# Two wide cross-attentions whose probabilities are turned by a DMA transpose, and smaller sums and weights in two small attention layers

## The reference, cut to what matters

```python
# l1x (8 key heads, each used twice)          # l3x
q = x @ Wq                                    # q = rmsnorm(x @ Wq, gq); k = rmsnorm(ctx @ Wk, gk)
scores = q @ k.T / sqrt(128)
attn = softmax(scores)                        # 128 x 128 for each batch and head
out = (attn @ v) @ Wo
```

```python
q = rope(x @ Wq + bq); k = rope(x @ Wk + bk); v = x @ Wv + bv
att = softmax(where(mask, einsum('bhgnd,bhsd->bhns', qg, k) / sqrt(d), -inf))
y = (att @ v) @ Wo + bo
```

## Time and profile before

| | us |
|---|---|
| median of 3 runs | 3186.46 (3185.35 to 3189.64) |
| profiled execution | 3178.78 |
| its span | 3177.0 |
| busy: PE, DVE, ACT, POOL | 2808.8, 2260.2, 1880.5, 1712.1 |

### The profile page before, as it was taken

How to read it: one execution, slowest core, us unless ns; L and a number is a source line. 1 busy time by engine, 2 the same in 40 slices (tenths; PEclk the granted TensorE clock), 3 DMA queues, 4 the chain that set the end, 5 groups by cost and what they waited for, 6 DMA issues and landing times. The chain is left out here.

```text
span 3177.0 us, 72083 instructions
## 1 busy us (share of the span) xinstructions
PE 2808.8 (88%) x25739; PEld 2153.6 (68%) x25739; DVE 2260.2 (71%) x5489; ACT 1880.5 (59%) x3629; POOL 1712.1 (54%) x1840
## 2 busy tenths in 40 slices
PE   7969999798999885896787899899999799998998
PEld 5757775456888565674565555688888677776665
DVE  5567764675888632885786677677777688888787
ACT  3346763355667422564676556466666588886675
POOL 2122211223555455554874376688888598887800
PEclk9989999799999976998899999999999999999999
DMA  4010001000000444000001632000000000001000
GB/s 165 1 23 12 13 11 67 7 1 8 10 7 5 140 119 97 6 6 23 16 16 28 241 92 69 3 1 0 0 0 0 6 9 5 5 5 47 24 1 27
DMA packets 94943, 104.66 MB, mean 33 GB/s; under 512 B 40492, under 2 KB 81900, under 8 KB 91759
## 3 DMA queue, kind: packets, MB, share of 16 engines
q1 hardware_dynamic: 90104, 96.09, 9.7%
q0 software_dynamic: 4608, 5.57, 1.1%
HBM read 80.84 MB, written 13.71 MB: 30 GB/s over the span
## 5 line engine op out<-in xcount | busy, mean ns | idle before, releaser
L2232 PE MATMUL bank<-l3a_ln_xnT,far 128*128 128x128 f16 x3072 | 194.4, 220 | 1.8 <-POOL l3a_ln_xnT L2046 1.8
L2232 PEld LDWEIGHTS bank<-l3a_ln_xnT,far 128*128 128x128 f16 x3072 | 181.7, 99 | 3.3 <-POOL l3a_ln_xnT L2046 2.2
L877 PE MATMUL bank<-l2f_xnT,l2f_wi 128*128 128x512 f16 x672 | 156.5, 381 | 7.0 <-POOLq L741 6.4
L3569 PE MATMUL bank<-l0x_v,l0x_pT 128*128 128x128 f32 x1024 | 134.7, 280 | 3.2 <-ACT l0x_pT L3997 1.5
L3569 PEld LDWEIGHTS bank<-l0x_v,l0x_pT 128*128 128x128 f32 x1024 | 127.7, 193 | 13.8 <-issue 4.7
L1226 PE MATMUL bank<-l3f_xnT,near 128*128 128x512 f16 x480 | 120.6, 389 | 6.9 <-DVE l3f_xnT L1011 3.5
L3163 POOL TENSOR_TENSOR l1x_prob<-l1x_prob,l1x_srec 128x512 f32<-128x512 f32 x64 | 66.6, 1041 | 105.7 <-DVE l1x_srec L2926 105.7
L1241 PE MATMUL bank<-near,l3f_h 128*128 128x256 f16 x960 | 119.0, 274 | 4.7 <-DVE l3f_h L1016 2.1
L877 PEld LDWEIGHTS bank<-l2f_xnT,l2f_wi 128*128 128x128 f16 x672 | 65.2, 98 | 77.8 <-POOLq L741 9.9
L1241 PEld LDWEIGHTS bank<-near,l3f_h 128*128 128x128 f16 x960 | 94.0, 98 | 33.8 <-DVE l3f_h L1016 4.0
L3857 DVE TENSOR_REDUCE l0x_smax<-bank 128x4 f32<-128x512 f32 x128 | 86.2, 685 | 32.7 <-PE bank L3511 30.5
(11 more groups left out here) (743 smaller groups left out, 9404.7 us busy)
## 6 DMA issues: line engine op xcount, KB each, us to landing
far<-in_l1f_in SPq DMA_DIRECT2D x32, 256.0 KB, 3.9
l2f_front<-l2f_shares SPq DMA_DIRECT2D x5, 1024.0 KB, 4.4
sums<-near SPq DMA_DIRECT2D x2, 2176.0 KB, 18.7
far<-in_l1f_down SPq DMA_DIRECT2D x32, 128.0 KB, 4.2
far<-sums SPq DMA_DIRECT2D x8, 512.0 KB, 7.4
l2f_wi<-in_l2f_in SPq DMA_DIRECT2D x14, 256.0 KB, 6.1
far<-l0x_kT SPq DMA_DIRECT2D x64, 48.0 KB
far<-l2x_kT SPq DMA_DIRECT2D x32, 96.0 KB
```

The costliest lines, as they stand in the source:

```text
L877: last = nc.tensor.matmul(bank[:, :], wi16[n % 2][p][:, a, k, :], xnT[q][:, k, 512 * g:512 * g + 512], start=(k + p + q == 0), stop=(k == ...
L2232: last = nc.tensor.matmul(bank[:, P * j:P * j + P], w(k, 512 * c + P * j, P, p), norm.xnT[u][q][:, k, :], start=(k + p + q == 0), stop=(k ...
L3569: last = nc.tensor.matmul(b_o[:, at:at + P], pT[f % 3][:, j, :], v_all[b % NV][:, hv:hv + P], start=True, stop=True)
```

## The change

In both wide layers the probabilities stay the way they lie and are split before they are turned: `p16` holds upper and lower halves side by side (128 x 1024 float16), and SP issues one DMA transpose a chunk, of all eight blocks, from `p16` to `pT`, both with two buffers. TensorE's four float32 transposes and their PSUM bank go.

In l1x the split is made from `prob` in SBUF: ScalarE rounds (`upper_probs`), GpSimd subtracts (`lower_probs`), VectorE's subtraction goes. In l3x the exponentials go to PSUM bank 6 (`b_p`), one bank for all chunks, and give their row sums by the accumulator output; VectorE takes reciprocals, multiplies inside the bank, ScalarE rounds and VectorE subtracts from the bank; GpSimd's `divide` and VectorE's sum go. The exponentials of a chunk now wait until the chunk before has been split.

In l1a the 16 query heads' weights and bias are summed to 4 before use, so 192 columns are projected, and the rotation is three instructions. In l2x the reciprocals, the products and the offsets of the two halves are one instruction each instead of two.

In the diff, the pieces are in the order of the code: buffers, SP, TensorE, VectorE, ScalarE, GpSimd, then `small_attention_layer`.

```diff
-        b_p, b_kT = (core.bank[6:8], None) if merged else (core.bank[6:7] * 2, core.bank[7])
+        b_p, b_kT = core.bank[6:8]
-        q32, prob = sb("q32", [P, 512]), two("prob")
+        q32, prob = sb("q32", [P, 512]), two("prob") if merged else [b_p, b_p]
-        pT = [two(f"pT{u}", 512, F16) for u in range(2)]
+        p16 = [sb(f"p16{u}", [P, 2 * HC, P], F16) for u in range(2)]
+        pT = [sb(f"pT{u}", [P, 2 * HC, P], F16) for u in range(2)]
...
+                    if pr:
+                        b, u, c_, f = pr
+                        sp.wait_ge(p_split, f + 1)
+                        sp.sem_inc(p_cleared, 1)
+                        since(sp, o_made, f - 1)
+                        sp.sem_inc(p_cleared, 1)
+                        sp.dma_start_transpose(pT[c_ % 2][:, :, :], p16[c_ % 2][:, :, :].rearrange("p h k -> p (h k)")
+                                               ).then_inc(p_turned[c_ % 2], 16)
...
                 def heads_out(it):
                     b, u, c_, f = it
-                    pe.wait_ge(pT_lo, f + 1)
+                    pe.wait_ge(p_turned[c_ % 2], turns(b, c_) + 16)
...
+                    nc.vector.reciprocal(srec[c_ % 2][:, :], ssum[c_ % 2][:, :])
+                    dve.drain()
+                    nc.vector.tensor_tensor(heads(b_p[:, :]), heads(b_p[:, :]),
+                                            srec[c_ % 2][:, :].unsqueeze(2).to_broadcast(wide), ALU.mult
+                                            ).then_inc(p_ready, 1)
...
                     else:
                         kk, kt = behind(b, u, c_, K_K, NC), behind(b, u, c_, K_T, NC)
+                        if pr:
+                            lower_probs(pr)
                         if sc:
                             negated_max(sc)
...
-                        if pr:
-                            keep_probs(pr)
                         if kt:
                             query_squares(kt)
...
                 def exponentials(it):
                     b, u, c_, f = it
                     act.wait_ge(d_ready if merged else less_ready, f + 1)
-                    since(act, p_turned, f - 1)
+                    since(act, p_split, f - 1 if merged else f)
...
-                        last = nc.scalar.activation(prob[c_ % 2][:, at], b_s[:, at], ACT.Exp,
-                                                    bias=less[c_ % 2][:, j:j + 1], scale=q_rr[c_ % 2][:, j:j + 1])
+                        last = nc.scalar.activation(b_p[:, at], b_s[:, at], ACT.Exp,
+                                                    bias=less[c_ % 2][:, j:j + 1], scale=q_rr[c_ % 2][:, j:j + 1],
+                                                    accum_out=ssum[c_ % 2][:, j:j + 1])
...
+                def upper_probs(it):
+                    b, u, c_, f = it
+                    act.wait_ge(p_ready, f + 1)
+                    since(act, p_turned[c_ % 2], turns(b, c_))
+                    nc.scalar.copy(p16[c_ % 2][:, 0:HC, :], heads(prob[c_ % 2][:, :])).then_inc(p_hi, 1)
...
+                        if pr:
+                            lower_probs(pr)
                         if ex:
                             divide(ex)
...
-    QW = 384 if causal else D
+    QW = {"summed": 192, "grouped": 384}.get(kind, D)
...
+                def sum_groups(to, w):
+                    nc.vector.tensor_reduce(to[:, 0:64].rearrange("p (h d) -> p h d", h=4),
+                                            w[:, 0:D].rearrange("p (h g d) -> p h d g", h=4, g=4), AX.X, ALU.add)
+                    nc.vector.tensor_copy(to[:, 64:], w[:, D:])
...
-                    for i, (tok, ready) in enumerate(((q_tok[b % 2], q_ready), (k_tok[b % 2], k_ready))):
-                        nc.vector.tensor_tensor(tok[:, :, :], four(raws[b % 2][:, :])[:, i, :, :], sb_[:, i, :, :], ALU.add
-                                                ).then_inc(ready, 1)
+                    nc.vector.tensor_tensor(tok[b % 2][:, :, :].rearrange("p (a h) d -> p a h d", a=2),
+                                            four(raws[b % 2][:, :]), sb_, ALU.add).then_inc(q_ready, 1)
```

More of the change, by code:

```diff
@@ L2662, in context_attention_layer @@
         two = lambda n, w=512, dtype=F32: [sb(f"{n}{i}", [P, w], dtype) for i in range(2)]
-        q32, prob = sb("q32", [P, 512]), two("prob")
+        q32, prob = sb("q32", [P, 512]), two("prob") if merged else [b_p, b_p]
         qT = [two(f"qT{u}", 512, F16) for u in range(2)]
-        pT = [two(f"pT{u}", 512, F16) for u in range(2)]
+        p16 = [sb(f"p16{u}", [P, 2 * HC, P], F16) for u in range(2)]
+        pT = [sb(f"pT{u}", [P, 2 * HC, P], F16) for u in range(2)]
+        p_hi, p_split, p_cleared = sem("p_hi"), sem("p_split"), sem("p_cleared")
+        c_freed = sem("c_freed")
+        p_turned = [sem(f"p_turned{u}") for u in range(2)]
         oT = [two(f"oT{u}", 512, F16) for u in range(2)]
-        smax, ssum = sb("smax", [P, HC]), sb("ssum", [P, HC])
+        smax, ssum = sb("smax", [P, HC]), two("ssum", HC)
         srec = two("srec", HC)
@@ L2725, in _, with slot @@
                 load(1, 1)
-                with sp.Fori(1, NB // 2) as i:
-                    for u in range(2):
-                        sp.wait_ge(c_split, 2 * i + u - 1)
-                        load(2 * i + u, u)
+                def slot(b, u, c_):
+                    pr = behind(b, u, c_, K_P, NC)
+                    if c_ == 0 and behind(b, u, c_, 0, NC) and not (isinstance(b, int) and b < 2):
+                        sp.wait_ge(c_split, b - 1)
+                        sp.sem_inc(c_freed, 1)
+                        load(b, u)
+                    if pr:
[6 more added lines that the diff above has]
+                                               ).then_inc(p_turned[c_ % 2], 16)
+                run_slots(sp, slot, NC, 2, K_O)
             @block.tensor
@@ L2739, in merge @@
                         last.then_inc(m_made, 1)
-                def turn_probs(it):
-                    b, u, c_, f = it
-                    pe.wait_ge(p_ready, f + 1)
-                    since(pe, pT_lo, f - 1 if merged else f)
-                    for j in range(HC):
-                        last = nc.tensor.transpose(b_p[c_ % 2][:, P * j:P * j + P], prob[c_ % 2][:, P * j:P * j + P],
-                                                   core.ident[:, :])
-                    last.then_inc(p_turned, 1)
                 def squares(it):
@@ L2819, in heads_out @@
                     for p, q in HALVES:
-                        last = nc.tensor.matmul(b_o[:, :], c16[u][p][:, :], pT[c_ % 2][q][:, :],
+                        last = nc.tensor.matmul(b_o[:, :], c16[u][p][:, :],
+                                                pT[c_ % 2][:, HC * q:HC * q + HC, :].rearrange("p h k -> p (h k)"),
                                                 start=(p + q == 0), stop=(p == 1))
@@ L3130, in slot @@
                         if pr:
[L3131 removed]
+                            upper_probs(pr)
                     else:
@@ L3165, in divide, with lower_probs @@
                                             ).then_inc(p_ready, 1)
+                def lower_probs(it):
+                    b, u, c_, f = it
+                    pool.wait_ge(p_hi, f + 1)
+                    nc.gpsimd.tensor_tensor(p16[c_ % 2][:, HC:, :], heads(prob[c_ % 2][:, :]), p16[c_ % 2][:, 0:HC, :],
+                                            ALU.subtract).then_inc(p_split, 1)
                 def split_squares(it):
@@ L3368, in small_attention_layer @@
         if kind != "axial":
-            raws = [sb(f"raw{u}", [P, 512 if split else 384]) for u in range(2)]
+            raws = [sb(f"raw{u}", [P, 512 if split else QW]) for u in range(2)]
         if kind in ("grouped", "split"):
@@ L3639, in weights_part @@
                         centre(keys, 32)
+                    if kind == "summed":
+                        for k in range(KD):
+                            sum_groups(wide_w["q"][:, k, :], weights["q"][:, k, :])
                     dve.drain().then_inc(centred, 1)
@@ L3871, in keep_out @@
                     first = n * (g % R) if rounds > 1 else 0
[L3872 to L3874 removed]
+                    o = b_o[:, 0:n * W].rearrange("p (h a w) -> p h a w", h=n, a=parts)
+                    nc.vector.reciprocal(orec[:, 0:n, :], o[:, :, :, HD])
                     dve.drain()
```

107 lines of the change are left out of this document (46 added, 61 removed).

## The result

| | us |
|---|---|
| before, median of 4 runs beside it | 3185.90 (3175.82 to 3189.64) |
| after, median of 4 runs | 3237.93 (3232.92 to 3241.9) |
| ratio | 1.0168, 95% interval 1.0140 to 1.0195 |
| profiled execution after, its span | 3238.48, 3236.7 |

The changed kernel is 52 us slower. Forecast were 3236, with a range of 3160 to 3325, and "slower" with 0.81.

A forecast was written before the change was run, and what follows sets the result against it. It took TensorE to bound l1x and ScalarE, with all four engines 86 to 94% busy, to be critical in l3x. l3x +75, l1x -12, l1a -7, l2x -6 gave +50 on 3186.46: 3236 us, range 3160 to 3325.

The forecast's parts named there:

- l3x, ScalarE and VectorE: In l3x, ScalarE's exponentials wait 1.75 us more behind VectorE's subtraction and maximum; 7.27 us a chunk, +75 us with accumulator.
- The accumulator: Accumulator output of l3x's exponentials: +10 us, between free and 29, since summed beside a pass that runs anyway.
- The term of the waits: In l3x, 1.75 us more wait before exponentials, the 0.73 for transposes gone: 1.02 a chunk, +65 us over 64 chunks.
- l1x: the mechanism: In l1x, transposes leave full TensorE, part returns as a wait for the layer norm's lower half: -12 us.
- -31 for the transposes: In l1x, 64 float32 transposes of 0.49 us leave TensorE, the bound engine: 31 us gained.
- +19 for the norm's half: In l1x, GpSimd's new instruction delays the layer norm's lower half, so TensorE's first projection waits 1.16 us in 16 batches.
- The DMA: Transposing DMA of 256 KB lands in 3.9 us, up to 14.4 if serial; at 3.9 it does not bound l1x.
- DMA + 4.0: In l1x, the ring that closes over two chunks takes the DMA's time plus 4.0 us: 3.95 a chunk.
- the point from which it decides: DMA time from which its ring bounds l1x: 2 x 4.77 - 4.0 = 5.5 us.
- rival of a partly serial DMA: DMA takes 7.2 us, l1x 5.6 a chunk, +53 instead of -12; total +115, 3301 us; chance 0.13.
- The serial estimate of 10.5 us: Eight blocks transposed one after another by DMA: l1x 7.2 us a chunk, some 158 us more than before.
- Small layers: l1a -7 us by a narrower projection, l2x -6 by merged instructions; together -13, between 0 and -19.
- TensorE's clock: Rival: in l3x the clock falls to 1.2 GHz at 74% busy, 226 us longer, 3462; chance 0.04.

The follow-up runs named there:

- max_first: Changed kernel, but VectorE in l3x makes maximum and bias before subtracting the rounded probabilities from the bank; 3195.22 us, ratio 1.0032 to the kernel before.
- dve_sums: Changed kernel, but l3x's exponentials have no accumulator output and VectorE reduces the bank for the row sums; 3225.89 us, ratio 1.0147 to the kernel before.
- norm_early: Changed kernel, but GpSimd in l1x makes the next batch's layer norm lower half ahead of its division; 3218.45 us, ratio 1.0120 to the kernel before.
- l1x_old: Changed kernel with only l1x put back to its form before the change; 3254.56 us, ratio 1.0204 to the kernel before.
- small_old: Changed kernel with all small attention layers put back to their form before the change; 3247.73 us, ratio 1.0196 to the kernel before.
- twice: Changed kernel with every transposing DMA preceded by an identical, waited-for one into an unread buffer; 3323.47 us, ratio 1.0442 to the kernel before.

## Why the prediction was right

**l3x, ScalarE and VectorE: right.** It said 1.75 us more between rounding and exponentials, and 7.27 a chunk without accumulators. The distance is 2.19 where 2.24 was put together from rows of before, and the wait that goes (0.73) and the one that comes (1.60) are where it put them. Its own arithmetic closes: ScalarE's 5.52, with 0.38 for the accumulators and 1.60 of wait, is 7.50, and 7.48 was measured. max_first shows the order as the cause of 44 us: the instructions are the same and only VectorE's queue differs. dve_sums has 7.21 a chunk without accumulators, close to the 7.27, but with a longer VectorE slot.

**The accumulator: undersized.** +10 was taken between 0 and 29, with the reason that the sum is made beside a pass that runs anyway. That reason failed: the reading is an instruction of its own behind each activation. It measures 0.38 us a chunk, 24 over the layer, near the upper bound. The term was 14 us too small. The term of the waits was about as much too large: without the accumulators' 0.38 a chunk grew by 7.48 - 0.38 - 6.30 = 0.80 us, 51 us in 64, where 1.02 and 65 were forecast (the chunk of before was taken as 6.25 where it is 6.30, so 0.05 of the 0.22 is that). That l3x came out at +77 against +75 is therefore luck: two errors of some 14 us cancel.

**l1x: the mechanism right, both terms too large.** -31 for the transposes is -23.6 (330.4 to 306.8), which norm_early shows alone. In the middle of the layer it is 0.45 a chunk, 29 us in 64; part of the rest goes at the layer's end, where TensorE waits 2.9 us for the last transposes in norm_early. +19 for the norm's half is +16.8. The sum is -6.8 against -12.

**The DMA: right where it mattered.** 3.1 us for 3.9, DMA + 4.5 for DMA + 4.0, and the point from which it decides is 2 x 4.57 - 4.5 = 4.6 us, not 5.5. Twice the landing time goes beyond it, and l1x loses 81 us. So the rival of a partly serial DMA had its place right, and it fell on the duration. The serial estimate of 10.5 us, from the 1309 ns of the Trainium skill's "VectorE: DVE Perf Modes", section "The three transpose paths", is refuted for this form, eight blocks in one instruction: 3.1 us. By the Trainium skill's page "Advanced Engine Details and Errata", section "X-Bar Transpose (TRN2)", transposing DMAs are as fast as ordinary ones. The trace agrees as far as it goes: 256 KB transposed from SBUF to SBUF land after 3.1 us, and 256 KB of weights loaded the ordinary way after 3.9; no run has an ordinary move by the same route.

**Small layers: right in sign, too large.** -13 was forecast, between 0 and -19; undone, they cost 9 us. l1a is -7.8 in the mean (-7 forecast). The 54 matmuls of 10.3 us are now 48 of 5.4. l2x is -4.0 (-6 forecast), but l2f gives 3.5 back, which no step of the prediction had; over the eleven executions it is -2.8 and +2.7.

**TensorE's clock: nearly right.** No stretch of l3x fell to 1.2 GHz for long, but there are short ones (a mean of 0.97 in 2560 to 2860, where it was 1.00 before). The timeline of TensorE and a window over the same place, after the change:

```profile
2705.39 0.82 PE L2797 MATMUL bank<-near,l3x_cT 128*128 128x512 f16 x3 [1.93 <-DVE l3x_k_tok L2977]
...
2707.25 2.77 PE L2841 MATMUL bank<-near,l3x_oT 128*128 128x256 f16 x12
...
2714.18 1.47 PE L2841 MATMUL bank<-near,l3x_oT 128*128 128x256 f16 x12
```
```profile
2706.70:2710.10 3.40, 3.40 (x18) 2.27 (x17) 2.80 (x8) 3.33 (x8) 1.75 (x3) 0.52 0.00 0
```

TensorE had been idle for 1.93 us shortly before; the group of twelve then takes 2.77 us instead of 1.47, at half the clock, and then it is back. TensorE is not what bounds there, so it costs little: a chunk takes 7.48 us in each of the five executions with this l3x (after, l1x_old, small_old, norm_early, twice).

## What to carry to other kernels

When a buffer is written over within one slot, add up the whole way round: what the writer must wait for, and what stands ahead of that in the queue of the engine that frees it. Here two calls in another order were worth 44 us, and one GpSimd instruction moved ahead of two others 17 us. Relieving a full engine pays only if the loop that takes its place is shorter; and an instruction added to an engine that is not full can still cost nearly its whole length if it stands ahead of an operand that the loop waits for.

## What the runs showed of the hardware that was not expected

- The accumulator output of an activation is a second instruction (ACTIVATION_READ_ACCUMULATOR, 198 ns); start to start it adds 0.09 us to each activation: 0.44 us from one to the next, where four without it took 1.38.
- Activations of 128x128 into PSUM have a mean of 427 ns, into SBUF 461.
- A transposing DMA of eight 128x128 blocks of 2 bytes, SBUF to SBUF, lands after 3.1 us and holds SP's queue for 1.23 to 1.25 us.
- A two-input VectorE instruction of 512 columns takes 0.69 us with one input in PSUM, and 1.31 in the mean with both in SBUF beside a busy GpSimd; with both in SBUF and GpSimd idle it takes 0.68 to 0.69.
- The same code of l1a took 134.8 to 142.2 us, with the granted clock between 0.87 and 0.81.
